# Differential attention: the two groups of four tile transposes joined into one group of eight, consumers one step later

## The reference, cut to what matters

```python
Q1, Q2 = (Q[..., :dh], Q[..., dh:])
K1, K2 = (K[..., :dh], K[..., dh:])
lam = (lam1 - lam2 + LAMBDA_INIT)[None, :, None, None]
A1 = jnp.einsum('bhqd,bhkd->bhqk', Q1, K1) * scaling
A2 = jnp.einsum('bhqd,bhkd->bhqk', Q2, K2) * scaling
attn = jax.nn.softmax(A1, axis=-1) - lam * jax.nn.softmax(A2, axis=-1)
O = jnp.einsum('bhqk,bhkd->bhqd', attn, V)
rms = jnp.sqrt(jnp.mean(O * O, axis=-1, keepdims=True) + EPS)
O = O / rms * rms_scale * (1.0 - LAMBDA_INIT)
return jnp.einsum('bne,de->bnd', O.transpose(0, 2, 1, 3).reshape(B, N, -1), Wo)
```

## Time and profile before

| | us |
|---|---|
| runs (3) | 1960.73, 1969.68, 1974.17 |
| median | 1969.68 |
| profiled execution, its own time | 1975.89 |
| its span, first to last instruction | 1973.2 |
| mean granted TensorE clock, share of full | 0.949 |

### The profile page before, as it was taken

The page is one execution under the profiler, slowest core; times in us unless marked ns, Lnnn a source line. Parts: engine busy times, 40 slices in busy tenths (PEclk is TensorE's granted clock), DMA queues, the critical chain, the costliest instruction groups (busy, mean ns, idle before and its releaser), DMA issues. The chain is left out here.

```text
span 1973.2 us, 34447 instructions
## 1 busy us (share of the span) xinstructions
PE 1748.1 (89%) x13171; PEld 1432.4 (73%) x13199; DVE 1442.3 (73%) x2911; ACT 1152.1 (58%) x2340; POOL 1038.0 (53%) x998
## 2 busy tenths in 40 slices
PE   6999999999999999899699699964798558999997
PEld 4888888888888888787567577753577445666675
DVE  6888888888888888534587677857777488777772
ACT  4677766666666667455367565542333344666665
POOL 4888999999999998920312134425257530110111
PEclk9999999999999999999899899966799878999999
DMA  3000000001000000000000000002045300000000
GB/s 89 14 1 14 1 14 1 14 1 36 1 1 1 1 1 1 28 1 1 20 17 17 0 2 1 2 22 70 22 107 134 77 14 1 1 1 1 2 2 23
DMA packets 52068, 37.44 MB, mean 19 GB/s; under 512 B 7528, under 2 KB 45832, under 8 KB 51904
## 3 DMA queue, kind: packets, MB, share of 16 engines
q1 hardware_dynamic: 45216, 30.53, 5.3%
q0 software_dynamic: 5632, 4.20, 1.5%
q10 hardware_dynamic: 1056, 0.52, 0.1%
HBM read 29.99 MB, written 5.24 MB: 18 GB/s over the span
## 5 line engine op out<-in xcount | busy, mean ns | idle before, releaser
L753 POOL TENSOR_TENSOR dtl<-dts,dth 128x512 fp32r<-128x512 f32 x256 | 346.8, 1355 | 20.5
L683 DVE TENSOR_REDUCE nm<-PS 128x1 f32<-128x1024 f32 x256 | 311.1, 1216 | 18.5 <-PE PS L203 17.7
L1884 ACT ACTIVATE ET_a<-PS 128x256 f32<-128x256 f32 (+2 forms) x512 | 221.7, 496 | 124.8 <-PE PS L1783 76.5
L751 POOL CAST dth<-dts 128x512 fp32r<-128x512 f32 x256 | 239.7, 936 | 56.2 <-ACT dts L610 55.1
L201 PE MATMUL PS<-xh,yh 128*128 128x512 f32 x512 | 225.4, 440 | 11.3 <-ACT G L603 5.7
L144 PE MATMUL PS<-C,XN 128*128 128x128 f32 x1120 | 177.6, 284 | 38.6 <-DVE XN L196 37.0
L203 PE MATMUL PS<-xh,yl 128*128 128x512 f32 x512 | 204.4, 399 | 0.0
L202 PE MATMUL PS<-xl,yh 128*128 128x512 f32 x512 | 204.2, 399 | 0.0
L603 ACT ACTIVATE XNT<-PS,nm 128x1024 f32<-128x1024 f32 x128 | 142.8, 1116 | 92.7 <-DVE nm L683 92.5
L1703 POOL TENSOR_SCALAR_AFFINE_SELECT ET_a<-ET_a 128x1024 f32<-128x1024 f32 x32 | 34.9, 1092 | 305.9 <-ACT ET_a L1884 305.9
L610 ACT ACTIVATE dts<-PS 128x512 f32<-128x512 f32 x256 | 152.8, 599 | 51.0 <-POOL dtl L753 50.9
(11 more groups left out here) (419 smaller groups left out, 4711.6 us busy)
## 6 DMA issues: line engine op xcount, KB each, us to landing
e_wg<-in_WgT SPq DMA_DIRECT2D x16, 256.0 KB
e_wu<-in_WuT SPq DMA_DIRECT2D x16, 256.0 KB
e_wd<-in_WdT SPq DMA_DIRECT2D x16, 256.0 KB
X<-in_L_attn_X SPq DMA_DIRECT2D x2, 512.0 KB, 4.5
wqn<-in_L_attn_Wq SPq DMA_DIRECT2D x8, 128.0 KB, 2.2
wkn<-in_L_attn_Wk SPq DMA_DIRECT2D x8, 128.0 KB, 2.5
wvn<-in_L_attn_Wv SPq DMA_DIRECT2D x8, 128.0 KB, 2.6
won<-in_WoT SPq DMA_DIRECT2D x8, 128.0 KB, 2.6
```

Of the source, the lines that this page charges most:

```text
L683: e.tensor_reduce(self.nm[:, half, i:i + 1], self.S[half], AX.X, MAX, negate=True).then_inc(*self.top.up((g, half)))
L751: e.tensor_copy(hi, src).then_inc(*ts.up((g, g4, "h")))
L753: e.tensor_tensor(lo, src, f(hi), SUB).then_inc(*ts.up((g, g4, "l")))
L1884: e.activation(dst, src, ACT.Exp, scale=self.SC, bias=0.0).then_inc(*self.ex.up(it))
```

## The change

The eight transposes of a tile now stand together at the end of a TensorE step, half 0 then half 1, behind `meet`; before, half 0 stood ahead of `scores(g, 0)`. The copies on ScalarE are both of tile g-3 (half 0, square, half 1), the splits on POOL both of tile g-3. `meet` goes from g-4 to g-5, `gather` to odd steps, `weigh`, `square` and `take_out` from g-7 to g-8, TAIL from 7 to 8. POOL's `factors` is cut in two: the two operations on the sums of the exponentials run in the step with g mod 8 = 3, the rest in the step with g mod 8 = 0; `weights` and `add` move one step back. `exps` gains a wait on the first part of `factors` of two units before. The number of matmuls, transposes, copies and splits is unchanged.

```diff
@@ -350,7 +350,7 @@
     NG = 128
     S2 = 1.0 / math.sqrt(128)
     LI = 0.8 - 0.6 * math.exp(-0.3)
-    TAIL = 7
+    TAIL = 8
 
     def __init__(self, k, where, s, ffn):
         self.k, self.s, self.ffn = k, s, ffn
@@ -391,7 +391,7 @@
         self.jobs[2] = ("prep", 0)
         use = list(first)
         for g in range(NG + self.TAIL):
-            use += [("uo", g - 7)] if 0 <= g - 7 < NG else []
+            use += [("uo", g - 8)] if 0 <= g - 8 < NG else []
             use += [self.jobs[g]] if g in self.jobs else []
         self.before = {b: a for a, b in zip(use, use[1:])}
         self.first = first
@@ -410,8 +410,7 @@
         self.recip, self.ratio, self.combined = k.sig("sum_recip", tiles), k.sig("ratio", tiles), k.sig("combined", tiles)
         self.turned = k.sig("d_turned", grid(tiles, range(2)))
         self.copied = k.sig("dt_copied", grid(tiles, range(2)))
-        self.t_split = k.sig("dt_split", [(g, n, x) for g, n in [(0, 0)] + [y for g in range(1, NG) for y in ((g - 1, 1), (g, 0))] + [(NG - 1, 1)]
-                                          for x in "hl"])
+        self.t_split = k.sig("dt_split", grid(tiles, range(2), "hl"))
         self.met = k.sig("tokens_met", grid(range(NG // 2), range(2)))
         self.z_high, self.z_low = k.sig("z_high", range(NG // 2)), k.sig("z_low", range(NG // 2))
         self.squared, self.u_out = k.sig("o_squared", tiles), k.sig("u_out", tiles)
@@ -550,10 +549,8 @@
             if g == 0:
                 q.wait_ge(self.p_low, (0, "m"))
                 s.turn(e, q, 2)
-            if 0 <= g - 7 < self.NG:
-                weigh(g - 7)
-            if mid:
-                turn(g - 2, 0)
+            if 0 <= g - 8 < self.NG:
+                weigh(g - 8)
             if live:
                 scores(g, 0)
             if g == 0:
@@ -562,14 +559,15 @@
                 q.wait_ge(s.low, 3)
             if g in self.jobs:
                 run(self.jobs[g])
-            if 0 <= g - 4 < self.NG:
-                meet((g - 4) // 2, g % 2)
+            if 0 <= g - 5 < self.NG:
+                meet(*divmod(g - 5, 2))
             if mid:
+                turn(g - 2, 0)
                 turn(g - 2, 1)
             if g in (self.NG, self.NG + 1):
                 for m in (0, 1):
                     ffn.gated(e, q, "silu", 0, 2 * (g - self.NG) + m)
-            elif g == self.NG + 3:
+            elif g == self.NG + 4:
                 for m in (0, 1):
                     ffn.gated(e, q, "mul", 0, m)
 
@@ -600,6 +598,8 @@
             q.wait_ge(self.top, (g, half))
             if g >= 2:
                 q.wait_ge(self.combined, g - 2)
+            if u >= 2:
+                q.wait_ge(self.factor, (u - 2, 0))
             e.activation(self.E[g % 2][:, half, :], self.S[half], ACT.Exp, bias=self.nm[:, half, i:i + 1], scale=1.0,
                          accum_out=self.ss[:, u % 2, half, i:i + 1]).then_inc(*self.exped.up((g, half)))
 
@@ -627,14 +627,14 @@
         for g in range(self.NG + self.TAIL + 2):
             if 0 <= g - 1 < self.NG:
                 exps(g - 1, 0)
-            if g % 2 == 0 and 0 <= g // 2 - 3 < self.NG // 2:
-                gather(g // 2 - 3)
+            if g % 2 and 0 <= (g - 7) // 2 < self.NG // 2:
+                gather((g - 7) // 2)
+            if 0 <= g - 3 < self.NG:
+                turn(g - 3, 0)
+            if 0 <= g - 8 < self.NG:
+                square(g - 8)
             if 0 <= g - 3 < self.NG:
                 turn(g - 3, 1)
-            if 0 <= g - 7 < self.NG:
-                square(g - 7)
-            if 0 <= g - 2 < self.NG:
-                turn(g - 2, 0)
             if g < self.NG:
                 exps(g, 1)
             if g in self.jobs:
@@ -701,12 +701,12 @@
         for g in range(self.NG + self.TAIL + 2):
             if 0 <= g - 1 < self.NG:
                 share(g - 1)
-            if g % 2 == 0 and 0 <= g // 2 - 3 < self.NG // 2:
-                gather(g // 2 - 3)
+            if g % 2 and 0 <= (g - 7) // 2 < self.NG // 2:
+                gather((g - 7) // 2)
             if g < self.NG:
                 top(g, 1)
-            if 0 <= g - 7 < self.NG:
-                take_out(g - 7)
+            if 0 <= g - 8 < self.NG:
+                take_out(g - 8)
             if 0 <= g - 1 < self.NG:
                 self.combine(e, q, g - 1)
             if g < self.NG:
@@ -752,15 +752,18 @@
             q.wait_ge(ts, (g, g4, "h"))
             e.tensor_tensor(lo, src, f(hi), SUB).then_inc(*ts.up((g, g4, "l")))
 
-        def factors(u):
+        def factors(u, first):
 
             s1, a_, b_ = self.ss[:, u % 2, 0, :], self.fa[:, u % 2, :], self.fb[:, u % 2, :]
             fs = self.factor
+            if first:
+                q.wait_ge(self.exped, (8 * u + 7, 0))
+                e.tensor_tensor(a_, s1, s1, MUL).then_inc(*fs.up((u, 0)))
+                q.wait_ge(fs, (u, 0))
+                e.tensor_scalar(a_, a_, 1e-5, None, MUL).then_inc(*fs.up((u, 1)))
+                return
             q.wait_ge(self.squared, 8 * u + 7)
-            q.wait_ge(self.exped, (8 * u + 7, 0))
-            e.tensor_tensor(a_, s1, s1, MUL).then_inc(*fs.up((u, 0)))
-            q.wait_ge(fs, (u, 0))
-            e.tensor_scalar(a_, a_, 1e-5, None, MUL).then_inc(*fs.up((u, 1)))
+            q.wait_ge(fs, (u, 1))
             e.tensor_scalar(b_, self.sqs[:, u % 2, :], 1.0 / 256, None, MUL).then_inc(*fs.up((u, 2)))
             q.wait_ge(fs, (u, 2))
             e.tensor_tensor(b_, a_, b_, ADD).then_inc(*fs.up((u, 3)))
@@ -789,20 +792,22 @@
         weights(0)
         s.split_w(e, q)
         for g in range(self.NG + 3):
-            if g >= 15 and g % 8 == 7 and g < self.NG:
-                factors((g - 15) // 8)
+            if g >= 16 and g % 8 == 0:
+                factors((g - 16) // 8, False)
+            if g >= 11 and g % 8 == 3:
+                factors((g - 11) // 8, True)
             if 0 <= g - 3 < self.NG:
+                split(g - 3, 0)
                 split(g - 3, 1)
-            if 0 <= g - 2 < self.NG:
-                split(g - 2, 0)
-            if g % 16 == 7 and g // 16 + 1 < self.H:
+            if g % 16 == 8 and g // 16 + 1 < self.H:
                 weights(g // 16 + 1)
-            if g >= 16 and g % 8 in (0, 1) and g < self.NG:
-                add((g - 16) // 8, g % 8)
+            if g % 8 in (1, 2) and 17 <= g < self.NG:
+                add((g - 17) // 8, g % 8 - 1)
         self.ffn.split_of(e, q, "g1")
         for u in (self.U - 2, self.U - 1):
             if u == self.U - 1:
-                factors(u)
+                factors(u, True)
+                factors(u, False)
             add(u, 0)
             add(u, 1)
```

## The result

The changed kernel takes 1983.89 us (median of 4 runs, 1982.53 to 1984.90) beside 1966.38 us for the kernel before (4 runs, 1960.73 to 1974.17). The ratio is 1.0065, 95% interval 1.004 to 1.009. In a second comparison it was 1.0073 (1.0053 to 1.0092). So it is some 13 us slower. The two profiled executions lie closer together: 1982.53 us against 1975.89, spans 1980.5 and 1973.2.

A forecast was written before the change was run, and what follows sets the result against it. PE's own instruction stream was taken as the bound. Terms -1.3 + 6 - 4.8 + 2 = +1.9 us on the profiled 1975.89 gave 1977.8, or 1971.6 as a median, put at 1972; range 1961 to 1984.

The forecast's parts named there:

- rival B: Y product: POOL's new timing lengthens VectorE's combine, binding in most of 64 y steps; +20 us, 1990 us, chance 0.09.
- the likeliest case: Whole kernel: time the same within 1% (20 us), chance 0.89.
- (a): Joining the transpose groups in each PE step: a rounding gain, -1.3 us (0 to -2.6).
- (b): Scores of half 0 and y product fall due 0.43 us earlier, so PE waits more: +6 us (2 to 10).
- (c): POOL's burst comes a step later against y jobs, so five 0.95 us waits nearly vanish: -4.8 us (0 if still late).
- (d): Meet one step later uses older splits, but PE waits for POOL nowhere in the stretch: gain 0.
- (e): Weigh, square, take_out, add and second part of factors move together; weights nearer prep, cover 4 us: 0.
- (f): New wait of exps on an operation POOL does five steps earlier: 0, at most 2 us of an idling engine.
- (g): End of the stage: POOL has more left to split and reaches the feed-forward weights later: +2 us (0 to 3).
- The wait at 807: PE's wait of 2.06 us at 807.17, near the stage's end, forecast to go since meet asks for an older split.
- Rival C: PE clock over the loop: longer transpose groups drop it to 0.97 on average; +23 us, 1993 us, chance 0.03.

The follow-up runs named there:

- e5: Changed kernel with half 0's four transposes moved from the step's end to between the scores of half 0 and the job; loop 714.7 us, ratio 1.0045.
- e2: Changed kernel with POOL's two adds per unit moved from steps 1 and 2 of eight to 4 and 5; loop 708.4 us, ratio 1.0034.
- e8: Kernel before with only weigh, square, take_out, weights and adds one step later and factors cut in two; loop 710.6 us, ratio 1.0026.
- e1: Changed kernel with the first four feed-forward activations on ScalarE one step later, behind a gather; loop 717.0 us, ratio 1.0062.
- e10: Kernel before with only POOL's adds moved from steps 0 and 1 of eight to 4 and 5; loop 709.1 us, ratio 1.0038.
- e7: Changed kernel with adds in steps 4 and 5, output-weight scalings in step 4 of sixteen, feed-forward activations one step later; loop 710.6 us, ratio 1.0046.

## Why the prediction was right and where it was wrong

The measured 1983.9 lies at the upper end of the range, 12 us above the forecast of 1972, and it is inside by luck: the range reached that far only because half of rival B had been added, and B did not come as it was described. It is a change within 1%, as the likeliest case said, but a real loss: +6.6 us from profile to profile where +1.9 was summed, and +13 by the ratio. Two of the signs that were named failed: the period is 99.22 us, above 98.8, and the combines got longer on the mean, which was to show the forecast wrong.

(a) **Joining**: right. A group of eight is 0.87 us, a plain step 5.633 instead of 5.640, about -0.7 us over the loop's 116 steps.

(b) **Cover lost**: mechanism, places and size were right. In the steady periods the waits outside the burst's step grew from 0.54 to 1.22 us, 0.68 where I took 1.0. But the early periods have no more slack, as I had supposed: they cost most (2.07 us the first, in which the exponentials come later as well: in step 20 it ends at 2.47 us of the step, before at 1.36). Summed over all steps of the loop outside the burst it is about +6.9 against +6. The two errors cancel. The place is the y product more than the scores of half 0, and e5 shows that the second binds as soon as the first is covered.

(c) **POOL's burst, -4.8 us: the step that failed.** I reckoned with POOL's lateness only and gave it 0.7 us more. The wait was not relieved but changed its path: before, the combine ran first and POOL's lateness reached TensorE over the copy of dts (0.97 us a period). After, the add runs first and VectorE's lateness reaches it over the row maximum and the exponential (1.39). Both waits come in five periods, so that is 5 x 0.42 = +2.1 instead of -4.8. e2, which moves the adds, brings that step back to its plain length, and e8, which shifts POOL without joining, has 1.27 in it. I had written that it could be late all the same (0), and in rival B that longer combines could bind. The adds of 2.88 us in the earlier trace rows were the sign: I took them as the price of an add, and they were an add of 1.9 us held up by a combine.

(a) to (c) make -0.7 + 6.9 + 2.1 = 8.3 us, the loop's loss. The miss of the sum is (c).

(d), (e), (f): no wait of TensorE for POOL, the prep or the weights appeared between 100 and 800 us, as said.

(g) **The end**: the first cast of the feed-forward weights is at 826.17 (before 817.79), 2.1 us later once the 6.3 us of the later step 127 are taken off, as I had said, and the tail's end only 0.3 instead of 2. The wait at 807 is gone as said, but another of 2.71 at 826.57 that I had not seen came; e1 shows its cause. I moved gather in thought and did not ask what else stands by step number in ScalarE's tail.

Start: I said 0. Step 9 begins 2.3 us earlier (1.1 in the second profile), untested.

Rival B's mechanism, longer combines, came true in part (mean 1739 to 1791 ns): it costs at the scores of half 0 in one step of sixteen, not in most y steps. Rival C is refuted: groups of 0.87 us keep the clock at 1.00 over 700 us, against the rule of the Trainium skill ("TensorE: Matmul & The Clock Gate", part 4) that stood for it.

**Open.** By ratio 13 us are lost, and by the traces 8.3 in the loop, less 1 to 2 ahead of it. Over 63 executions of before, time falls by about 1.1 us for each 0.001 of the mean granted clock of the whole run (0.945 to 0.956); at equal clock after still is 12 to 14 us slower on the mean. Before's profiled execution lies 5 us above that line, and e10 shows the same gap (+1.0 of loop, ratio 1.0038). The rest of the program, behind the feed-forward block of the first layer, doesn't hold it: it takes 1025.2 us in before's profile at a clock of 0.949, and 1024.8 to 1025.9 in after, e2, e5 and e7 at 0.948 to 0.950. So before's one profile may be some 5 us slow ahead of that point, and the loss against before larger than 8.3. A second profile of before would tell; there is none. Joining and meet's lag were never run apart with everything else equal, so their 5.8 us are not divided.

## What to carry to other kernels

Before an operation of GpSimd is moved by a step, lay it beside VectorE's instructions with two SBUF inputs: if it now starts first, VectorE pays what is left of it, and VectorE may be the one nearest to TensorE's path. Read an unusually long instruction as a wait in disguise and find the one whose end it follows by a constant. And when a stage's lag grows, list everything that is placed by step number, its tail too.

## What I had not expected of the hardware

The exclusion is exact: between 100 and 800 us the combine ends 1.07 to 1.09 us behind the POOL instruction that held it, adds and splits alike (after 394.71 + 1.39 = 396.10, the split of 393.73 + 1.29 = 395.02), while row maxima from PSUM kept 1.21 to 1.23 us beside the same add. Not every POOL instruction holds a combine: beside the 1.67 us operation of `factors` on 8 columns (L768) all 14 kept 1.27 or 1.28 us. And a POOL cast of 0.61 us takes up to 1.6 when a combine holds it.
